# The first microseconds of an attention and experts block: silu from Exp, the first root on ScalarE, the upper halves ahead of the decay

## Chip, cores and metric

One core of one Trainium2 chip. The metric is the device time of one execution in microseconds (us), the median of several runs. A profiled execution gives the trace; its span goes from the first to the last instruction.

## The reference

`x` is 8 sequences of 256 tokens with 128 features. A modulation is computed from a condition `c` (8 x 128), and everything else is one attention and one mixture of experts:

```python
mod = (silu(c) @ wmod).reshape(8, 6, 1, 128)
sa, ca, ga, sb, cb, gb = mod[:, 0], ..., mod[:, 5]
h = layernorm(x) * (1 + ca) + sa
# attention: 16 heads of 8; the scores are multiplied by a decay before the softmax
lag = abs(i - j); scores = (q @ k.T) * scale * exp(-alpha * lag)
x = x + ga * (softmax(scores) @ v @ Wo.T + bo)
h = layernorm(x) * (1 + cb) + sb
# 16 experts, 2 per token, and one shared
x = x + gb * (routed_experts(h) + shared_expert(h))
```

The layer norm needs 1 / sqrt(variance + eps), silu is c / (1 + exp(-c)).

## The kernel before

The kernel is written for each engine by hand: five programs (SP for the loads, GpSimd, ScalarE, VectorE, TensorE) that run beside each other, each in its own written order, and meet only in semaphores. An engine does nothing behind a wait until that wait is over.

**Chunks.** The 2048 tokens are four chunks of 512 (two sequences each). Attention runs over the chunks one after the other, 32 head steps each in groups of four: TensorE makes scores from `qk_st` (L979), VectorE multiplies them with `decay` and takes the maximum (`head`, L736, L741), GpSimd forms maximum minus score (L306), TensorE turns it, ScalarE takes Exp (L420), and TensorE multiplies with the values in `v_one` (L1009). The experts follow, over the same four chunks, in units of two experts.

**Upper and lower halves.** Queries and keys are split into a rounded upper part and the remainder, and the four combinations of them lie in `qk_st`, which SP fills by copies from `qk` (`stack_slot`, L151, issued at L153), 64 in all. For the first four heads of the first chunk there is no time for copies: `w_first` has its rows arranged so that one matmul gives all combinations, ScalarE writes the upper halves to `act_hi` (`first_hi`, L562), and VectorE subtracts and writes `qk_st` directly (`first_lo`, L836).

**The start.** The first chunk is treated one sequence at a time. "First rows" are the two tiles of 128 tokens of the first sequence (tiles 0 and 1), "second rows" those of the second (tiles 2 and 3). The order of the work is:

- SP issues ten loads (`load`, L173 to L185): the first rows' `x_all`, `ct_sb` (the condition), `wmod_sb` for the first two modulations, the identity `id_f`, the second rows' `x_all`, `wf_sb`, `decay` (which holds the lags at first), the rest of `wmod_sb`, `wa_sb` (attention weights), and the rest of `x_all`. ScalarE issues three small ones (L547 to L549): `vf_sb`, `alpha_sb`, `vec_sb`.
- VectorE clears `attn_t`, on which TensorE runs warm-up matmuls (`warm`, L1160). It takes statistics and means of the first rows (`stats_first`, L819), normalises them to `xn` (`xn_first`, L829), copies the first two modulations out of PSUM (L853, L854), makes `nalpha` (L856), and does the statistics of the second rows. Then come `first_lo` for the first sequence, `xn` of the second rows, and three heads.
- GpSimd clears and marks the first half of `v_one` (`clear_values`, L330: one memset over all, two strided ones that put the 1.0 by which the sums are formed), then makes the root of the first rows, `(variance + eps) ** -0.5` (`root_first`, L324, L326 and L328), that of the second rows, the shift for later rows (`ln1_shift`), and, once the second rows' `xn` is done, the second half of `v_one`. After that its loop over the head steps begins.
- ScalarE takes silu of the condition (L551), loads the table set that holds Ln and Exp, runs an Exp on `spare` (L555), shifts and scales the transposed rows to `h_t` (`h_first`, L557), takes Exp of the lags (L578, in place in `decay`), and then the upper halves of the first sequence, the second sequence's `h_t`, and so on.
- TensorE runs eight warm-ups, the two modulations from `silu_c`, two more warm-ups, the transposes of `xn` (`lnt_first`), three warm-ups, the matmuls with `wf_sb` (`first`), four warm-ups, the scores, the second rows' transposes, and the projections with `wa_sb` (`project_seq`).

Two places show how a wait stands in front of a later one. ScalarE's order of the first sequence, and the load semaphore that both the lags and `alpha` count on:

```python
act_e.wait_ge(s["ld_decay"], 32)          # L576: lags and alpha, 16 each
act_e.wait_ge(s["nalpha_ok"], 1)
nc.scalar.activation(decay[:], decay[:], ACT.Exp, scale=nalpha[:, 0:1])
act_e.wait_ge(s["ld_vf"], 16)
first_hi(0)
```

VectorE waits for the same count of 32 ahead of `nalpha` (L855).

Of the kernel before, what the change touches and what calls it, by code (L numbers as in the profile page):

```python
# [50 lines left out]
def build(nc, x, x_t, c_t, w_first, v_first, w_attn, vecs, alpha, w_r, w_gu, w_d, w_mod, lag, ident, out):  # L51
# [3 lines left out]
    with ExitStack() as ctx:  # L55
        def sb(name, shape, dt=F32):
            return ctx.enter_context(nc.sbuf_tensor(name, shape, dt))

        def sem(name):
# [16 lines left out]
        wmod_sb = sb("wmod_sb", [P, 6, D])  # L76
        ct_sb, silu_c = sb("ct_sb", [P, NB]), sb("silu_c", [P, NB])
        mod_t = sb("mod_t", [P, 6, NB])
        gate_s, gate_m = sb("gate_s", [P, 2, NB]), sb("gate_m", [P, 2, NB])
        bo2, ga_bo = sb("bo2", [P, 1]), sb("ga_bo", [P, NB])  # L80
        nhalf, spare, eps = sb("nhalf", [P, TT]), sb("spare", [P, TT]), sb("eps", [P, 1])

# [43 lines left out]
        s = {n: sem(n) for n in (  # L126
            "ld_x0 ld_x0b ld_ct ld_id ld_vf ld_x xb_ok ld_mod ld_mod_b ld_first ld_attn ld_decay ld_ffn nalpha_ok decay_raw silu_ok modt_mm modt_ok modb_mm modb_ok "
            "stats_a mv_a vare_a rstd_a xn_a lnt_a h_a warm_ok first_mm first_hi first_ok bo_mm bo_ok gate_a gate_b gate_c gate_ok gabo_ok vone_ok pool_init eps_init lg_init whi_ok wlo_ok "
# [43 lines left out]
        def _(sp):  # L172
            def load(ap, dram, done):  # L173
                sp.dma_start(ap, dram).then_inc(s[done], 16)  # L174

            load(x_all[:, 0:BPC, :], x_v[:, 0:BPC, :], "ld_x0")
            load(ct_sb[:], c_t, "ld_ct")
            load(wmod_sb[:, SA:CA1 + 1, :], w_mod[:, SA:CA1 + 1, :], "ld_mod")
            load(id_f[:], ident, "ld_id")
            load(x_all[:, BPC:TT, :], x_v[:, BPC:TT, :], "ld_x0b")  # L180
            load(wf_sb[:], w_first, "ld_first")
            load(decay[:], lag, "ld_decay")
            load(wmod_sb[:, GA_IN:, :], w_mod[:, GA_IN:, :], "ld_mod_b")
            load(wa_sb[:], w_attn, "ld_attn")
            load(x_all[:, TT:, :], x_v[:, TT:, :], "ld_x")  # L185
# [84 lines left out]
        def _(pool):  # L270
# [11 lines left out]
            def ln1_shift(c):  # L282
                shift(c, mv, nmean, rstd, nmr, "mv_ok", "nmean_ok", "rstd_ok", "nmr_ok")
# [46 lines left out]
            def clear_values(k):  # L330
                nc.gpsimd.memset(v_one[:, k, :], 0.0).then_inc(s["pool_init"], 1)
                pool.wait_ge(s["pool_init"], 2 + k)
                cells = v_one[:, k, 0:TT * HEADS * VW].rearrange("p (t h a w) -> p t h a w", h=2, w=VW, t=TT)
                for h in range(2):
                    last = nc.gpsimd.memset(cells[:, :, h, :, VD + 1 - 2 * h:VD + 2 * HD - 2 * h:2], 1.0)
                last.then_inc(s["vone_ok"], 1)

            clear_values(0)
            root_first(slice(0, BPC), "mv_a", "vare_a", "rstd_a")
            root_first(slice(BPC, TT), "mv_ok", "vare_ok", "rstd_ok")  # L340
            ln1_shift(0)
            pool.wait_ge(s["xn_ok"], 1)
            clear_values(1)
            for i in range(NCHUNK):
# [15 lines left out]
        def _(act_e):  # L360
# [158 lines left out]
            def chunk(i):  # L519
                prev, nxt = i > 0, i < NCHUNK - 1  # L520
                for q in range(QUADS):
# [22 lines left out]
                    if (i, q) in SPLITS:  # L544
                        split(SPLITS.index((i, q)))

            act_e.dma_start(vf_sb[:], v_first).then_inc(s["ld_vf"], 16)  # L547
            act_e.dma_start(alpha_sb[:], alpha.to_broadcast([P, 1])).then_inc(s["ld_decay"], 16)
            act_e.dma_start(vec_sb[:], vecs).then_inc(s["ld_attn"], 16)  # L549
            act_e.wait_ge(s["ld_ct"], 16)  # L550
            nc.scalar.activation(silu_c[:], ct_sb[:], ACT.Silu).then_inc(s["silu_ok"], 1)  # L551
            act_e.wait_ge(s["pool_init"], 1)
            act_e.wait_ge(s["eps_init"], 1)
            nc.scalar.preload_act_table_set("natural_log_exp_and_others")
            nc.scalar.activation(spare[:], nhalf[:], ACT.Exp)  # L555

# [18 lines left out]
            h_first(0, "lnt_a", "h_a")  # L575
            act_e.wait_ge(s["ld_decay"], 32)  # L576
            act_e.wait_ge(s["nalpha_ok"], 1)
            nc.scalar.activation(decay[:], decay[:], ACT.Exp, scale=nalpha[:, 0:1]).then_inc(s["decay_raw"], 1)  # L578
            act_e.wait_ge(s["ld_vf"], 16)
            first_hi(0)  # L580
            h_first(1, "lnt_done", "h_ok")
# [59 lines left out]
        def _(dve):  # L641
# [174 lines left out]

            nc.vector.memset(attn_t[:], 0.0).then_inc(s["warm_ok"], 1)

# [23 lines left out]
            def qk_lo_seq(b, ready, done):  # L842
                for i in range(2):
# [4 lines left out]
                                                   ALU.subtract).then_inc(s[done], 1)  # L848

            stats_first(range(0, BPC), "ld_x0", "stats_a", "mv_a")  # L850
            xn_first(range(0, BPC), "rstd_a", "xn_a")
            dve.wait_ge(s["modt_mm"], 1)
            nc.vector.tensor_copy(mod_t[:, SA, :], ps_s[0][:, 0:NB]).then_inc(s["modt_ok"], 1)  # L853
            nc.vector.tensor_scalar(mod_t[:, CA1, :], ps_s[0][:, NB:2 * NB], 1.0, None, ALU.add).then_inc(s["modt_ok"], 1)  # L854
            dve.wait_ge(s["ld_decay"], 32)  # L855
            nc.vector.tensor_scalar(nalpha[:], alpha_sb[:], -1.0, None, ALU.mult).then_inc(s["nalpha_ok"], 1)  # L856
# [94 lines left out]
        def _(pe):  # L951
# [232 lines left out]

            warm(2)
            pe.wait_ge(s["ld_id"], 16)
# [143 lines left out]
```

## Time and profile before

| | |
|---|---|
| median of 3 runs | 238.72 us (238.61 to 238.99) |
| profiled execution | 238.33 us |
| its span | 236.5 us |
| instructions | 5820 |

The page counts busy time of each engine in the span, the chain that ended last by engine and line, and the load of the DMA engines. PE is TensorE's matmul, PEld its weight load, DVE is VectorE, ACT ScalarE, POOL GpSimd; an engine's name with a q is its queue of issues. All TensorE instructions have one line, L953, since a helper records them, so they are told apart by their operands.

### The profile page before, as it was taken

To read this page: it belongs to the slowest core of one execution; us is meant where nothing else is said; L and a number is where in the kernel's file an instruction comes from. 1 tells how busy PE (TensorE), PEld (TensorE's weight loads), DVE (VectorE), ACT (ScalarE), POOL (GpSimd) and SP (SyncE) were. 2 spreads that over 40 slices of the span, in tenths; PEclk is the share of its full clock that TensorE was granted. 3 is DMA by queue.
4 is the path that set the end of the run, shared out by engine and by line. 5 is a ranking of instruction groups with operands and counts; after the bars stand their busy time and mean duration, and the time that the engine had idled before them with its cause. 6 is when DMAs were issued, how large, how long until landed. Compare 5 with 4: busy or idle time off the path is not lost.

```text
span 236.5 us, 5820 instructions
## 1 busy us (share of the span) xinstructions
PE 225.0 (95%) x1828; PEld 166.0 (70%) x1828; DVE 189.9 (80%) x793; ACT 165.1 (70%) x335; POOL 181.5 (77%) x334
## 2 busy tenths in 40 slices
PE   7879999999999999999998999999999999999994
PEld 7767657665666676667666767677788887787882
DVE  3699897998998889899799988387756796966763
ACT  5558767699586999686975796776667659565550
POOL 6599898999897989989999989156486464666551
PEclk9999999999999999999999999999999999999999
DMA  5715845741008711017622540024323430045201
GB/s 143 225 46 123 245 162 136 198 113 47 4 15 198 186 63 36 0 29 198 176 81 96 196 136 0 4 91 133 111 81 127 127 98 0 0 135 198 95 26 44
DMA packets 16622, 24.38 MB, mean 103 GB/s; under 512 B 3344, under 2 KB 6544, under 8 KB 16464
## 3 DMA queue, kind: packets, MB, share of 16 engines
q1 hardware_dynamic: 16160, 24.01, 35.0%
q8 instruction: 15, 0.25, 0.4%
q14 instruction: 15, 0.12, 0.2%
q10 hardware_dynamic: 432, 0.01, 0.1%
HBM read 13.39 MB, written 1.18 MB: 62 GB/s over the span
## 4 chain that ended last, share of the span: by engine, by line
PE 61%; DVE 13%; ACT 11%; SPq 5%; issue 4%; DMA 3%; POOL 3%; DVEq 0%; ACTq 0%
PE bank L953 61%; DVE sc L741 5%; ACT pr L420 4%; SPq L153 4%; POOL sc L306 2%; ACT h_t L362 2%; DMA decay<-in_lag 1%; ACT xn L375 1%; DMA qk_st<-qk 1%; SPq L174 1%; DVE sc L917 1%; DVE qk_st L838 1%; DVE ex L702 1%; DVE mx L741 1%; DVE stats L644 1%
## 5 line engine op out<-in xcount | busy, mean ns | idle before, releaser
L306 POOL TENSOR_SCALAR sc<-sc,mx 128x256 f32<-128x256 f32 x256 | 121.3, 492 | 8.0 <-DVE mx L741 6.5
L741 DVE CUSTOM_DVE_ANT_0 sc<-bank,decay 128x256 f32<-128x256 f32 x256 | 91.0, 418 | 11.3 <-PE bank L953 11.1
L420 ACT ACTIVATE pr<-bank 128x512 f32<-128x512 f32 x128 | 69.2, 595 | 18.1 <-PE bank L953 18.1
L350 POOL TENSOR_TENSOR act_lo<-sc,act_hi 128x512 fp32r<-128x512 f32 x35 | 45.1, 1292 | 34.8 <-ACT act_hi L596 34.8
L953 PE MATMUL bank<-id_f,sc 128*128 128x128 f32 x512 | 69.1, 277 | 2.7 <-ACT pr L420 2.3
L953 PEld LDWEIGHTS bank<-id_f,sc 128*128 128x128 f32 x512 | 55.8, 141 | 16.4 <-issue 8.7
L911 DVE TENSOR_TENSOR pr<-bank,cwb 128x512 f32<-128x512 f32 x32 | 22.0, 688 | 15.6 <-PE bank L953 15.5
L953 PE MATMUL bank<-pr,v_one 128*32 128x256 f32 x512 | 34.3, 385 | 0.0
L605 ACT ACTIVATE bank<-bank 128x512 f32<-128x512 f32 x32 | 18.6, 582 | 20.5 <-PE bank L953 20.1
L917 DVE TENSOR_TENSOR sc<-pr,bank 128x512 f32<-128x512 f32 x36 | 24.7, 687 | 5.7 <-PE bank L953 2.4
L953 PE MATMUL bank<-h_hi,wgu_hi 128*128 128x512 f32 x72 | 28.8, 400 | 0.0
L953 PE MATMUL bank<-h_lo,wgu_hi 128*128 128x512 f32 x72 | 28.4, 395 | 0.0
L953 PE MATMUL bank<-h_hi,wgu_lo 128*128 128x512 f32 x72 | 28.4, 395 | 0.0
L596 ACT ACTIVATE act_hi<-sc 128x512 fp32r<-128x512 f32 x36 | 22.4, 623 | 2.9 <-DVE sc L917 2.9
L953 PEld LDWEIGHTS bank<-pr,v_one 128*32 128x32 f32 x512 | 13.3, 109 | 12.8 <-issue 4.9
L741 DVE DVE_READ_ACCUMULATOR2_ANT mx<- 128x1 f32 x256 | 21.0, 82 | 0.0
L953 PE MATMUL bank<-qk_st 32*128 32x256 f32 x256 | 16.2, 327 | 2.1 <-DVE mx L741 0.9
L953 PEld LDWEIGHTS bank<-h_hi,wgu_hi 128*128 128x128 f32 x72 | 13.5, 188 | 3.5 <-issue 0.4
L953 PEld LDWEIGHTS bank<-h_lo,wgu_hi 128*128 128x128 f32 x72 | 13.5, 187 | 3.3
L953 PEld LDWEIGHTS bank<-h_hi,wgu_lo 128*128 128x128 f32 x72 | 13.5, 188 | 3.1
L953 PEld LDWEIGHTS bank<-qk_st 32*128 32x128 f32 x256 | 9.8, 183 | 7.9 <-issue 5.8
L953 PE MATMUL bank<-act_hi,wd_hi 128*128 128x512 f32 x36 | 15.1, 419 | 0.0
(114 smaller groups left out, 267.2 us busy)
## 6 DMA issues: line engine op xcount, KB each, us to landing
cwb<-cw_dram SPq DMA_DIRECT2D x64, 128.0 KB, 3.0
qk_st<-qk SPq DMA_DIRECT2D x56, 128.0 KB, 2.7
wgu_sb<-in_w_gu SPq DMA_DIRECT2D x1, 1152.0 KB, 5.9
wgu_sb<-in_x_t SPq DMA_DIRECT2D x4, 256.0 KB, 3.8
x_all<-in_x SPq DMA_DIRECT2D x1, 768.0 KB, 6.0
o_sum<-o_t SPq DMA_DIRECT2D x6, 128.0 KB, 2.2
o_val<-o_t SPq DMA_DIRECT2D x6, 128.0 KB, 2.2
out_dram<-wgu_sb SPq DMA_DIRECT2D x3, 256.0 KB, 3.1
```

The source lines that it names most:

```text
L153: eng.dma_start(qk_st[slot:P:SLOTS, :, g, cols].bitcast(F32), qk[32 * g:32 * g + 32, bq:bk + 1:bk - bq, cols].bitcast(F32)).then_inc(done ...
L174: sp.dma_start(ap, dram).then_inc(s[done], 16)
L306: last = nc.gpsimd.tensor_scalar(sc[:, n % RING, t, :], sc[:, n % RING, t, :], -1.0, mx[:, n % RING, t:t + 1], ALU.mult, ALU.add)
L350: nc.gpsimd.tensor_tensor(act_lo[:, (i * NU + u) % FR, :], act[:, (i * NU + u) % FR, :], act_hi[:, (i * NU + u) % FR, :].bitcast(F32), ALU ...
L362: return nc.scalar.activation(dst, src, ACT.Identity, bias=bias[:, at:at + 1], scale=scale[:, at:at + 1])
L420: nc.scalar.activation(pr[:, n % RING, :, :].rearrange("p a b -> p (a b)"), turn_bank(i, n)[:], ACT.Exp, scale=-1.0).then_inc(s["exp_done" ...
L596: nc.scalar.activation(act_hi[:, (i * NU + u) % FR, :], act[:, (i * NU + u) % FR, :], ACT.Copy).then_inc(s["ahi_ok"], 1)
L605: nc.scalar.activation(gate[:], gate[:], ACT.Silu).then_inc(s["silu_done"], 1)
L741: last = nc.vector.tensor_tensor_reduce(sc[:, n % RING, t, :], ps_s[n % SB][:, t * SEQ:t * SEQ + SEQ], decay[:, t, :], float(HD) ** -0.5, ...
L911: nc.vector.tensor_tensor(gate_u[:, n % 2, :], up[:], cwb[:, u, :], ALU.mult).then_inc(s["mul_done"], 1)
L917: nc.vector.tensor_tensor(act[:, r, :], gate_u[:, n % 2, :], (gate if u < ROUTED else up)[:], ALU.mult).then_inc(s["act_ok"], 1)
L953: return nc.tensor.matmul(o, l, r, start=start, stop=stop, skip_group_check=not check, is_transpose=transpose or None)
```

## The change

Seven edits, all in the first part of the kernel:

- **silu from Exp.** ScalarE makes `c_den = exp(-c)`; VectorE adds 1, inverts and multiplies by `c` (`silu_of`, three small operations on 128 x 8 with a wait between each), between the first rows' means and their `xn`. The table set with Ln and Exp is loaded at the start; the load of the silu table and the Exp of `spare` at the start are gone.
- **The first rows' root** is made on ScalarE by Ln and Exp (`exp(-0.5 * ln(variance + eps))`).
- **GpSimd** marks `v_one` in a function of its own (`mark_sums`). It clears and marks the first half, waits for the first rows' `xn`, clears the second half, makes the second rows' root, marks the second half, and makes the shift.
- **Upper halves ahead of the decay** on ScalarE.
- **Loads.** `ct_sb` goes to ScalarE's queue, as its first; `vec_sb` to SP's; `wf_sb` goes ahead of the second rows' `x_all`, and `wa_sb` and `vec_sb` ahead of the rest of `wmod_sb`. ScalarE's other two loads come behind the table load in its program.
- **Waits.** `alpha` has a semaphore of its own, on which VectorE waits.
- **Warm-up.** `attn_t` is cleared over 128 of its 512 columns, and two warm-ups ahead of the transposes are gone.

```diff
             load(x_all[:, 0:BPC, :], x_v[:, 0:BPC, :], "ld_x0")
-            load(ct_sb[:], c_t, "ld_ct")
             load(wmod_sb[:, SA:CA1 + 1, :], w_mod[:, SA:CA1 + 1, :], "ld_mod")
             load(id_f[:], ident, "ld_id")
+            load(wf_sb[:], w_first, "ld_first")
             load(x_all[:, BPC:TT, :], x_v[:, BPC:TT, :], "ld_x0b")
-            load(wf_sb[:], w_first, "ld_first")
             load(decay[:], lag, "ld_decay")
+            load(wa_sb[:], w_attn, "ld_attn")
+            load(vec_sb[:], vecs, "ld_attn")
             load(wmod_sb[:, GA_IN:, :], w_mod[:, GA_IN:, :], "ld_mod_b")
-            load(wa_sb[:], w_attn, "ld_attn")
             load(x_all[:, TT:, :], x_v[:, TT:, :], "ld_x")
...
             def clear_values(k):
                 nc.gpsimd.memset(v_one[:, k, :], 0.0).then_inc(s["pool_init"], 1)
+
+            def mark_sums(k):
                 pool.wait_ge(s["pool_init"], 2 + k)
...
             clear_values(0)
-            root_first(slice(0, BPC), "mv_a", "vare_a", "rstd_a")
+            mark_sums(0)
+            pool.wait_ge(s["xn_a"], 1)
+            clear_values(1)
             root_first(slice(BPC, TT), "mv_ok", "vare_ok", "rstd_ok")
+            mark_sums(1)
             ln1_shift(0)
-            pool.wait_ge(s["xn_ok"], 1)
-            clear_values(1)
...
+            act_e.dma_start(ct_sb[:], c_t).then_inc(s["ld_ct"], 16)
+            nc.scalar.preload_act_table_set("natural_log_exp_and_others")
             act_e.dma_start(vf_sb[:], v_first).then_inc(s["ld_vf"], 16)
-            act_e.dma_start(alpha_sb[:], alpha.to_broadcast([P, 1])).then_inc(s["ld_decay"], 16)
-            act_e.dma_start(vec_sb[:], vecs).then_inc(s["ld_attn"], 16)
+            act_e.dma_start(alpha_sb[:], alpha.to_broadcast([P, 1])).then_inc(s["ld_alpha"], 16)
             act_e.wait_ge(s["ld_ct"], 16)
-            nc.scalar.activation(silu_c[:], ct_sb[:], ACT.Silu).then_inc(s["silu_ok"], 1)
-            act_e.wait_ge(s["pool_init"], 1)
+            nc.scalar.activation(c_den[:], ct_sb[:], ACT.Exp, scale=-1.0).then_inc(s["cexp_ok"], 1)
             act_e.wait_ge(s["eps_init"], 1)
-            nc.scalar.preload_act_table_set("natural_log_exp_and_others")
-            nc.scalar.activation(spare[:], nhalf[:], ACT.Exp)
+            act_e.wait_ge(s["mv_a"], 1)
+            nc.scalar.activation(var_e[:, 0:BPC], mv[:, 0:BPC, 1], ACT.Ln, bias=eps[:, 0:1], scale=1.0).then_inc(s["vare_a"], 1)
+            act_e.wait_ge(s["vare_a"], 1)
+            nc.scalar.activation(rstd[:, 0:BPC], var_e[:, 0:BPC], ACT.Exp, scale=-0.5).then_inc(s["rstd_a"], 1)
...
             h_first(0, "lnt_a", "h_a")
-            act_e.wait_ge(s["ld_decay"], 32)
+            act_e.wait_ge(s["ld_vf"], 16)
+            first_hi(0)
+            act_e.wait_ge(s["ld_decay"], 16)
             act_e.wait_ge(s["nalpha_ok"], 1)
             nc.scalar.activation(decay[:], decay[:], ACT.Exp, scale=nalpha[:, 0:1]).then_inc(s["decay_raw"], 1)
-            act_e.wait_ge(s["ld_vf"], 16)
-            first_hi(0)
             h_first(1, "lnt_done", "h_ok")
...
-            nc.vector.memset(attn_t[:], 0.0).then_inc(s["warm_ok"], 1)
+            nc.vector.memset(attn_t[:, 0:P], 0.0).then_inc(s["warm_ok"], 1)
...
+            def silu_of():
+                dve.wait_ge(s["cexp_ok"], 1)
+                nc.vector.tensor_scalar(c_den[:], c_den[:], 1.0, None, ALU.add).then_inc(s["cden_ok"], 1)
+                dve.wait_ge(s["cden_ok"], 1)
+                nc.vector.reciprocal(c_den[:], c_den[:]).then_inc(s["cinv_ok"], 1)
+                dve.wait_ge(s["cinv_ok"], 1)
+                nc.vector.tensor_tensor(silu_c[:], ct_sb[:], c_den[:], ALU.mult).then_inc(s["silu_ok"], 1)
+
             stats_first(range(0, BPC), "ld_x0", "stats_a", "mv_a")
+            silu_of()
             xn_first(range(0, BPC), "rstd_a", "xn_a")
...
-            dve.wait_ge(s["ld_decay"], 32)
+            dve.wait_ge(s["ld_alpha"], 16)
             nc.vector.tensor_scalar(nalpha[:], alpha_sb[:], -1.0, None, ALU.mult).then_inc(s["nalpha_ok"], 1)
...
-            warm(2)
             pe.wait_ge(s["ld_id"], 16)
             lnt_first(0, "xn_a", "lnt_a")
```

## Rows read from the trace of the kernel before

**Rows 1.** The page: granted clock in 40 slices, and the chain by engine.
```profile
PEclk9999999999999999999999999999999999999999
...
PE 61%; DVE 13%; ACT 11%; SPq 5%; issue 4%; DMA 3%; POOL 3%; DVEq 0%; ACTq 0%
```

**Rows 2.** The chain that ended last, in order of time: start us, us, what.
```profile
3.66 3.46 DMA decay<-in_lag
...
8.02 0.55 ACT act_hi L565
...
8.60 0.95 DVE qk_st L838 x2
...
24.46 2.79 DMA qk_st<-qk
```

**Rows 3.** Timeline, 1 to 6 us: start us, us, engine, line, operation, operands [idle before].
```profile
1.44 3.59 PE L953 MATMUL bank<-attn_t 128*128 128x128 f32 x16 [1.44 <-DVE attn_t L817]
...
2.14 1.28 ACT L551 ACT_TABLE_LOAD   x1 [2.14 <-issue]
...
2.78 0.65 POOL L335 MEMSET v_one<- 128x256 f32 x2
...
3.63 0.25 DVE L826 BATCH_NORM_AGGREGATE mv<-stats 128x2 f32<-128x6 f32 x2
...
3.99 0.21 ACT L551 ACTIVATE silu_c<-ct_sb 128x8 f32<-128x8 f32 x1 [0.56 <-DMA ct_sb<-in_c_t]
...
4.21 1.28 ACT L554 ACT_TABLE_LOAD   x1
4.25 0.73 POOL L328 TENSOR_TENSOR rstd<-var_e,nhalf 128x2 f32<-128x2 f32 x1
...
5.01 0.60 DVE L832 TENSOR_SCALAR xn<-x_all,mv,rstd 128x128 f32<-128x128 f32 x2 [1.13 <-POOL rstd L328]
...
5.51 0.20 ACT L555 ACTIVATE spare<-nhalf 128x4 f32<-128x4 f32 x1
```

**Rows 4.** The same timeline, 6 to 17 us.
```profile
6.27 0.56 ACT L362 ACTIVATE h_t<-bank,mod_t 128x256 f32<-128x256 f32 x1 [0.56 <-PE bank L953]
...
6.98 1.10 PE L953 MATMUL bank<-h_t,wf_sb 128*128 128x256 f32 x4
...
7.40 0.72 ACT L578 ACTIVATE decay<-decay,nalpha 128x512 f32<-128x512 f32 x1 [0.56 <-DVE nalpha L856]
...
8.07 0.19 POOL L326 TENSOR_SCALAR var_e<-mv 128x2 f32<-128x2 f32 x1 [3.09 <-DVE mv L826]
...
9.46 0.59 DVE L832 TENSOR_SCALAR xn<-x_all,mv,rstd 128x128 f32<-128x128 f32 x2
...
10.11 1.82 POOL L331 MEMSET v_one<- 128x2064 f32 x1 [0.51 <-DVE xn L832]
...
10.29 0.42 DVE L741 CUSTOM_DVE_ANT_0 sc<-bank,decay 128x256 f32<-128x256 f32 x1 [0.23 <-PE bank L953]
...
13.53 1.13 PE L953 MATMUL bank<-h_t,wa_sb 128*128 128x256 f32 x4 [1.20 <-DVE qk_st L838]
...
14.27 0.91 ACT L571 ACTIVATE qk<-bank,vec_sb 128x256 fp32r<-128x256 f32 x2 [1.31 <-PE bank L953]
...
16.51 0.94 POOL L306 TENSOR_SCALAR sc<-sc,mx 128x256 f32<-128x256 f32 x2 [0.23 <-DVE mx L741]
```

**Rows 5.** Three lines, each by itself: duration ns min/median/max, first and last start us.
```profile
L382 ACT ACTIVATE var_e<-mv,eps x6: 290/306/328, 20.0 to 136.6; 128x4 f32<-128x4 f32 x6
...
L723 DVE RECIPROCAL rz<-zs x2: 177/178/178, 104.0 to 135.3; 128x4 f32<-128x4 f32 x2
...
L888 DVE TENSOR_TENSOR gate_m<-mod_t,gate_s x1: 414/414/414, 23.2 to 23.2; 128x16 f32<-128x16 f32 x1
```

**Rows 6.** DMA issues of the first 25 us: KB each, us to landing.
```profile
x_all<-in_x SPq DMA_DIRECT2D x2, 128.0 KB, 2.5
...
alpha_sb<-in_alpha ACTq DMA_DIRECT2D x1, 0.5 KB, 2.6
```

More of the change, by code:

```diff
@@ L76, in build @@
         wmod_sb = sb("wmod_sb", [P, 6, D])
-        ct_sb, silu_c = sb("ct_sb", [P, NB]), sb("silu_c", [P, NB])
+        ct_sb, c_den, silu_c = sb("ct_sb", [P, NB]), sb("c_den", [P, NB]), sb("silu_c", [P, NB])
         mod_t = sb("mod_t", [P, 6, NB])
@@ L80, in build @@
         bo2, ga_bo = sb("bo2", [P, 1]), sb("ga_bo", [P, NB])
-        nhalf, spare, eps = sb("nhalf", [P, TT]), sb("spare", [P, TT]), sb("eps", [P, 1])
+        nhalf, eps = sb("nhalf", [P, TT]), sb("eps", [P, 1])
         x_all = sb("x_all", [P, NCHUNK * TT, D])
@@ L126, in build @@
         s = {n: sem(n) for n in (
-            "ld_x0 ld_x0b ld_ct ld_id ld_vf ld_x xb_ok ld_mod ld_mod_b ld_first ld_attn ld_decay ld_ffn nalpha_ok decay_raw silu_ok modt_mm modt_ok modb_mm modb_ok "
+            "ld_x0 ld_x0b ld_ct ld_alpha ld_id ld_vf ld_x xb_ok ld_mod ld_mod_b ld_first ld_attn ld_decay ld_ffn nalpha_ok decay_raw cexp_ok cden_ok cinv_ok silu_ok modt_mm modt_ok modb_mm modb_ok "
             "stats_a mv_a vare_a rstd_a xn_a lnt_a h_a warm_ok first_mm first_hi first_ok bo_mm bo_ok gate_a gate_b gate_c gate_ok gabo_ok vone_ok pool_init eps_init lg_init whi_ok wlo_ok "
```

## The prediction

> **What bounds the kernel now.** I read the page's chain first, to see which engine the time belongs to: 61% of the chain that ended last is TensorE's own work, at a granted clock that is full (2.4 GHz) in every one of the 40 slices [rows 1]. The change touches only the first 15 us or so, so the second view is the chain in order of time over the first 30 us [rows 2]. There the end is not set by TensorE: it runs through the landing of `decay` (issued 3.66, landed 7.12), the Exp of `decay` on ScalarE, the rounding to `act_hi` at 8.02, VectorE's two `qk_st` parts at 8.60 to 9.55, then (through the scores, the second rows' transposes, `h_t` and the rest of the second sequence) to a run of issues of `qk_st` copies on SP whose last one goes out at 24.46 and lands at 27.25. Behind that landing stands ScalarE's next `qk`, and from 28.66 TensorE itself is the chain. What is won ahead of 9.55 therefore moves the whole string, if each later link follows from the one before and not from something that stays put. Third, I read the timeline of each engine from 1 to 16 us, for what each instruction really waited for [rows 3, 4].
>
> **Part one: the first rows' root, and silu.** Before: VectorE's means end at 3.88 (3.63 + 0.25); GpSimd does the root in two instructions that end at 4.98, and VectorE starts `xn` at 5.01 [rows 3]. After: ScalarE does Ln and Exp. An Ln with its bias from memory takes 0.30 [rows 5], an Exp 0.20 (that of `spare`), and an engine follows its predecessor after some 0.03: 3.88 + 0.03 + 0.30 + 0.03 + 0.20 + 0.02 = 4.46. In VectorE's queue the three small operations of silu now stand ahead of `xn`. A small tensor_scalar or tensor_tensor isn't shown with GpSimd quiet and both operands in SBUF; from below I bound it by 0.15 (GpSimd's own 0.19 for the same size is near it), from above by the 0.41 that `gate_m` took beside a running GpSimd [rows 5]. Here GpSimd's marking has ended at 3.43 [rows 3], so I take 0.15, and 0.18 for the reciprocal [rows 5]: 3.91 + 0.15 + 0.03 + 0.18 + 0.03 + 0.15 = 4.45. The two strings end together, so `xn` starts at about 4.46 in place of 5.01: **0.55 earlier**. By the upper bound silu would end at 4.97 and this part would bring nearly nothing.
>
> Silu's input must be there. `ct_sb` moves to the head of ScalarE's queue (issue 0.72, in place of 1.23 on SP); ScalarE then has one table load of 1.28 and two issues of 0.45 before its Exp, which puts the Exp at 1.17 + 1.28 + 0.90 = 3.35 at the latest if nothing of this overlaps, and it ends by 3.6, ahead of 3.91. The second load of 1.28 (4.21 to 5.49) and the Exp of `spare` go, but ScalarE sat idle behind them until 6.27 [rows 3, 4], so they bring nothing by themselves: they are what allows ScalarE to do the root at all. The Trainium skill (ScalarE: Activation LUTs, section What ACT_TABLE_LOAD costs) adds a drain of about 1.38 us to each load of about 1.28. Here the Exp of `spare` started at 5.51, 0.02 after the load's end, so the trace shows no such drain; what it would cost is a rival below.
>
> Silu's result came at 4.20 and now comes at 4.45; TensorE was in its sixteen warm-up matmuls until 5.03 [rows 3], and with a clearing of `attn_t` a quarter as wide these start, and end, some 0.3 earlier. So the modulation's matmuls follow at about 4.55 and are done before `xn` is (5.06). They are covered; without the cover silu would show with 0.25. Two warm-up pairs of matmuls go ahead of the transposes; the wait there is for `xn`, so I cost their absence at nothing as long as the clock stays full, as it does now even across idle time [rows 1].
>
> **Part two: upper halves ahead of the decay.** Before, `h_t` began at 6.27; the matmuls with `wf_sb` began at 6.98; ScalarE took `decay` at 7.40 (it waited for the landing at 7.12) for 0.72 and could start `act_hi` only at 8.02 [rows 2, 4]. With `act_hi` first, its start is set by TensorE alone. The same pattern of matmuls with nothing in ScalarE's way stands at 13.53, with ScalarE's `qk` at 14.27: 0.74 from the first matmul to the taking [rows 4]. So 6.98 + 0.74 = 7.72 against 8.02: **0.30 earlier** by the swap alone. The matmuls need `wf_sb`, which is now issued two places earlier on SP, so it is no later. Together, `act_hi` starts at 8.02 - 0.55 - 0.30 = 7.17, and `qk_st` at 7.75 instead of 8.60: **0.85**.
>
> **What must not be late next.** `decay` now runs behind `act_hi`, at 8.17 to 8.89; VectorE's first head, which reads it, would start at 10.29 - 0.85 = 9.44, and ScalarE's second `h_t` later still, so 0.5 us of cover. Its load moves up one issue slot (about 0.5) with the same bytes ahead of it, so it lands between 6.6 and 7.12. The wait for `alpha` comes ahead of the second rows' statistics in VectorE's queue: issued at 1.65 or, behind the load, at 2.95, it takes 2.6 to land [rows 6] and so comes at 5.6 at the latest; before, that place waited until 7.12 for `decay`. The second `x_all` piece is issued at the same place as before, with `wf_sb` ahead of it instead of `ct_sb`: 2.67 + 2.5 = 5.2, and at most 0.6 more for the 124 KB extra at the rate of the rows before it. Statistics and means take 0.8, so means by 6.6.
>
> GpSimd: it waits for the first `xn` (5.06), clears for 1.82 (until 6.95), then var, 0.09 and the power, 0.19 + 0.09 + 0.73 [rows 3, 4]: the second root is ready at about 8.0. VectorE asks for it at 9.46 - 0.85 = 8.61, behind `qk_st`. Cover 0.6; beyond it each us of delay costs one. The marking (0.65) comes after it, next to VectorE's second `xn`. The queues: `vec_sb` goes from ScalarE's queue to SP's, and the attention weights pass the rest of the modulation's; they land near 8, and TensorE asks at 9.5. The modulation's rest lands about 0.5 later, some 7 us before it is used. The large `x_all` load keeps its place.
>
> GpSimd's second clearing, from 10.11 to 11.93, and its marking no longer stand ahead of the loop, so GpSimd's first head step can start near 10 instead of behind 12.5. I cost this at nothing: at 16.51 GpSimd had waited for VectorE [rows 4], so its lateness was made up by then.
>
> **Sum.** 0.55 + 0.30 = 0.85 off the chain. The profiled execution (238.33, span 236.5) would go to 237.48; it stands 0.39 below the median of the runs, so on the median 238.72 - 0.85 = 237.87, which I give as 237.9. A measurement of this kernel can tell about 0.2% (0.48 us) from no change.
>
> **Rivals.**
> *A, the gain is partly swallowed* (0.15). Silu's operations take the upper bound, or one link of the string to 27.25 hangs on something that stays put, such as the SP's issues being held by the DMA rings. For it: that string holds 16 copies, and the transfer of 2.79 is not TensorE's. Against: the copies' first wait is VectorE's result, which moves. With only part two left: 238.72 - 0.30 = 238.4.
> *B, the early GpSimd brings more* (0.05). If TensorE's first turns were held by GpSimd's late start rather than by VectorE, up to 0.5 more: 237.4.
> *C, ScalarE isn't ready* (0.03). If the first load blocked ScalarE for twice its 1.28, and the two issues came after, the Exp would run from 4.63 to 4.83, silu end at 5.40 and `xn` start at 5.41, 0.40 late; less the 0.30: 238.8. The drain rule of the Trainium skill quoted above would give 0.1 more than this. The start at 5.51 speaks against it.
> *D, slower: the second root comes late* (0.04). The place is GpSimd's clearing, now ahead of that root. It decides from 8.61 on, and the kernel is slower than before when the root passes 9.46. If the clearing were stretched beside VectorE as `gate_m` was (0.41 against 0.15, 2.7 times), it would take 4.9, the root would be ready at 11.1, and the time 238.72 + 1.65 = 240.4. Against: the clearing at 10.11 ran beside VectorE's heads and took the same 1.82 as the first.
> *E, the shifted start meets the long TensorE part badly* (0.03): the relative order of GpSimd and VectorE changes, up to 0.7 slower, 239.4. No row speaks for it.
>
> **How the numbers follow.** The forecast has 0.70: 237.5 to 238.2, nearly all of it faster by over 0.2%. Faster: 0.68 of it, B's 0.05, and 0.01 of A, 0.74. Same: the rest of A, C and 0.02 of the forecast, 0.19. Slower: D and E, 0.07. The range 237.1 to 238.6 leaves out D, E, C and the tails on both sides.
>
> **What would show it.** Right: one table load on ScalarE, Ln at about 3.9, `xn` at 4.4 to 4.6, `act_hi` at 7.1 to 7.3, `qk_st` at 7.7 to 7.8, the second `xn` near 8.6, the last first-chunk copy landing at 26.4, and every row behind it 0.85 earlier. Wrong: VectorE idle ahead of the second `xn` with GpSimd as releaser (D); the small operations at 0.3 or more each (A); a head that waits for `decay`; or a string that is 0.85 early at 10 us and on time at 27.

## The result and the profile after

| | before | after |
|---|---|---|
| median of 10 runs each | 238.74 us (238.23 to 239.53) | 237.81 us (237.45 to 238.48) |
| ratio | | 0.9958, 95% interval 0.9938 to 0.9978 |
| profiled execution, its span | 238.33, 236.5 | 237.55, 235.8 |

The change takes 0.93 us off the median; 0.85 was forecast. The whole interval lies beyond 0.2%. The sum came out, but not all of its terms did, so the profile after is read by its steps.

The page of the changed kernel, granted clock and chain (the answer to [rows 1]):

```profile
PEclk9999999999999999999999999999999999999999
...
PE 63%; DVE 13%; ACT 11%; SPq 4%; issue 3%; POOL 3%; DMA 1%; DVEq 0%; ACTq 0%
```

The timeline of the changed kernel, 1 to 10 us, rows of all engines in order of time (the answer to [rows 3, 4]):

```profile
1.04 3.78 PE L967 MATMUL bank<-attn_t 128*128 128x128 f32 x16 [1.04 <-DVE attn_t L822]
...
1.18 1.28 ACT L551 ACT_TABLE_LOAD   x1 [1.18 <-PEq L1336]
...
2.75 0.21 ACT L555 ACTIVATE c_den<-ct_sb 128x8 f32<-128x8 f32 x1 [0.29 <-DMA ct_sb<-in_c_t]
...
4.00 0.30 ACT L558 ACTIVATE var_e<-mv,eps 128x2 f32<-128x2 f32 x1 [1.04 <-DVE mv L831]
...
4.23 0.17 DVE L861 TENSOR_TENSOR silu_c<-ct_sb,c_den 128x8 f32<-128x8 f32 x1
...
4.51 0.93 PEld L967 LDWEIGHTS bank<-silu_c,wmod_sb 128*128 128x128 f32 x4
...
4.57 0.60 DVE L837 TENSOR_SCALAR xn<-x_all,mv,rstd 128x128 f32<-128x128 f32 x2 [0.17 <-ACT rstd L560]
...
5.22 1.82 POOL L331 MEMSET v_one<- 128x2064 f32 x1 [1.80 <-DVE xn L837]
...
5.39 0.49 PE L967 MATMUL bank<-id_f,xn 128*128 128x128 f32 x2
5.57 0.17 DVE L867 COPY mod_t<-bank 128x8 f32<-128x8 f32 x1 [0.41 <-PE bank L967]
...
5.98 0.56 ACT L365 ACTIVATE h_t<-bank,mod_t 128x256 f32<-128x256 f32 x1 [1.45 <-PE bank L967]
...
7.42 0.73 POOL L328 TENSOR_TENSOR rstd<-var_e,nhalf 128x2 f32<-128x2 f32 x1
7.46 1.02 ACT L570 ACTIVATE act_hi<-bank,vf_sb 128x256 fp32r<-128x256 f32 x2 [0.91 <-PE bank L967]
8.05 0.94 DVE L843 SCALAR_TENSOR_TENSOR qk_st<-bank,vf_sb,act_hi 128x256 fp32r<-128x256 f32 x2 [1.50 <-ACT act_hi L570]
8.37 0.71 ACT L585 ACTIVATE decay<-decay,nalpha 128x512 f32<-128x512 f32 x1
8.91 0.59 DVE L837 TENSOR_SCALAR xn<-x_all,mv,rstd 128x128 f32<-128x128 f32 x2
```

Two rows of the kernel before go beside these:

```profile
4.76 0.53 PEld L953 LDWEIGHTS bank<-silu_c,wmod_sb 128*128 128x128 f32 x4
...
5.76 0.41 PE L953 MATMUL bank<-id_f,xn 128*128 128x128 f32 x2
```

`xn` is 0.44 earlier, and `h_t` only 0.29. In between stand TensorE's matmuls for the modulation and its transposes of `xn`, and TensorE was still slow: the four weight loads for the modulation took 0.93, against 0.53 before, and VectorE's copy of the result waited 0.41 for them. But the modulation was not what `h_t` waited for. It was copied by 5.81, and the transposes ended at 5.88 (5.39 + 0.49), 0.10 ahead of `h_t`; before, they ended at 6.17, also 0.10 ahead. The transposes began only 0.37 earlier than before, 0.22 behind the end of `xn` in place of 0.14, while the modulation's last weight load ran until 5.44; and they took 0.49 in place of 0.41. `act_hi` is 0.56 earlier, `qk_st` 0.55.

The chain of the changed kernel in order of time (the answer to [rows 2]):

```profile
1.04 4.86 PE bank L967 x22
...
8.05 0.95 DVE qk_st L843 x2
...
24.01 2.91 DMA qk_st<-qk
```

`decay` has left the chain, and TensorE's own start, warm-up and modulations, has entered it. From `qk_st` on the string moved too, but less and less: 0.55 there, 0.45 at the last copy's issue (24.46 to 24.01), 0.33 at its landing (27.25 to 26.92). TensorE's last long piece began at 203.90 before and at 203.13 after, 0.77 earlier. Most of this extra arises far behind the change, at one instruction of VectorE. Before and after:

```profile
120.24 2.40 DVE L689 TENSOR_TENSOR h_lo<-h_t,h_hi 128x512 fp32r<-128x512 f32 x1
...
119.85 1.95 DVE L694 TENSOR_TENSOR h_lo<-h_t,h_hi 128x512 fp32r<-128x512 f32 x1
```

`h_lo`, a subtraction for the experts, starts 0.39 earlier and is 0.45 shorter; the head step behind it (122.56 and 121.90) is 0.66 earlier. The change does not touch this place. In the profiles of the twelve kernels below, `h_lo` took 1.50 to 2.07 in ten and 2.41 and 2.51 in two, e12 and e8, both with the new root. So it differs by profile and isn't shown to be a gain of the change. The last 0.1 appears near 157.

### The profile page after: what moved, and what is told of

Same layout as the page of the kernel before. It is cut to its first block, busy times and chain, and to the rows that moved or that the text cites. A ratio compares the mean times of both kernels' runs of the same rounds, so it can differ in the third digit from the quotient of the medians.

```text
span 235.8 us, 5813 instructions
## 1 busy us (share of the span) xinstructions
PE 224.9 (95%) x1824; PEld 166.1 (70%) x1824; DVE 189.5 (80%) x796; ACT 164.0 (70%) x335; POOL 180.6 (77%) x332
## 3 DMA queue, kind: packets, MB, share of 16 engines
q1 hardware_dynamic: 16160, 24.01, 35.7%
## 4 chain that ended last, share of the span: by engine, by line
PE 63%; DVE 13%; ACT 11%; SPq 4%; issue 3%; POOL 3%; DMA 1%; DVEq 0%; ACTq 0%
PE bank L967 63%; DVE sc L746 6%; ACT pr L423 4%; SPq L153 4%; POOL sc L306 2%; ACT h_t L365 2%; ACT xn L378 1%; DMA qk_st<-qk 1%; DVE sc L931 1%; DVE qk_st L843 1%; DVE ex L707 1%; DVE mx L746 1%; DVE stats L649 1%; DVE struck L719 1%; ACT L610 1%
## 5 line engine op out<-in xcount | busy, mean ns | idle before, releaser
L967 PEld LDWEIGHTS bank<-id_f,sc 128*128 128x128 f32 x512 | 55.7, 141 | 16.8 <-issue 8.7
```

The lines of the kernel that those rows point to most:

```text
L967: return nc.tensor.matmul(o, l, r, start=start, stop=stop, skip_group_check=not check, is_transpose=transpose or None)
```

## The experiments

Twelve kernels ran, four at a time on one chip, in 12 executions each. The table gives each against the kernel before on the same chip (medians of different chips are not compared) and, in us of its one profile, the start of `h_t`, `act_hi` and `qk_st` and the last tenth of a us in which the TensorE weight loads under way still took about 300 ns or more on average.

| kernel | median | ratio to before (95%) | range | `h_t`, `act_hi`, `qk_st` | slow until |
|---|---|---|---|---|---|
| e0_after | 237.59 | 0.9966 (0.9951 to 0.9981) | 237.27 to 238.39 | 6.10, 7.58, 8.18 | 5.8 |
| e1_decay_first | 237.86 | 0.9966 (0.9952 to 0.998) | 237.3 to 238.22 | 5.77, 7.74, 8.32 | 3.8 |
| e2_swap_only | 238.66 | 1.0002 (0.9987 to 1.0017) | 238.01 to 239.32 | 6.53, 8.01, 9.04 | 5.1 |
| e3_root_on_gpsimd | 238.55 | 0.9999 (0.9981 to 1.0017) | 237.73 to 239.22 | 6.62, 8.73, 9.33 | 10.2 |
| e7_old_warmup | 239.08 | 0.9999 (0.9981 to 1.0018) | 237.67 to 239.55 | 6.10, 7.58, 8.18 | 4.2 |
| e9_gpsimd_root_warm | 239.05 | 1.0012 (0.9988 to 1.0035) | 237.89 to 240.43 | 6.61, 8.09, 8.69 | 5.7 |
| e4_clear_twice | 239.46 | 1.0036 (1.0013 to 1.0059) | 238.93 to 244.27 | 6.16, 7.88, 8.48 | 7.0 |
| e8_qk_behind_exps | 237.86 | 0.9961 (0.9947 to 0.9975) | 237.52 to 238.26 | 6.09, 7.57, 8.17 | 5.9 |
| e11_full_clearing | 237.91 | 0.9968 (0.995 to 0.9985) | 237.31 to 238.54 | 6.38, 7.86, 8.46 | 5.8 |
| e12_two_warmups | 238.17 | 0.9994 (0.9972 to 1.0015) | 237.43 to 239.94 | 6.21, 7.69, 8.29 | 4.9 |
| e13_new_warmup_only | 238.48 | 1.0 (0.998 to 1.0019) | 237.81 to 239.82 | 6.29, 8.13, 8.71 | 5.3 |
| e14_old_warmup_again | 238.32 | 0.9998 (0.9983 to 1.0014) | 237.69 to 239.21 | 6.39, 7.87, 8.47 | 4.9 |

The kernel before had medians of 238.55, 238.9 and 238.57 on the three chips, with executions from 237.84 to 239.73.

### First four: the changed kernel again, the swap, the root

> The changed kernel itself, once more, beside the others. Theory 1 (TensorE's own clock): its first matmuls run at half speed until a moment that varies from execution to execution; in the first profile of the changed kernel the weight loads took 333 ns until about 5.3 us, so that the two modulations took 0.93 us in place of 0.51 and h_t came at 5.98 in place of 5.72. Then this execution need not show the same: with the rise at 4.7 or earlier h_t is at 5.7, with the rise at 5.3 it is at 5.98 again. Theory 2 (the earlier warm-up brought the modulations into the slow stretch, always): h_t at 5.98 again, the rise at 5.3. Time 237.8 by both.

Inconclusive between the two theories by itself: TensorE rose at 5.8, later still, and `h_t` came at 6.10. Here the slow stretch reached through the transposes:

```profile
5.34 0.67 PE L967 MATMUL bank<-id_f,xn 128*128 128x128 f32 x2
```

The kernel e1 has the same start on TensorE and decided it: there the loads took 192 ns from 4.1 on.

```diff
 h_first(0, "lnt_a", "h_a")
+act_e.wait_ge(s["ld_decay"], 16)
+act_e.wait_ge(s["nalpha_ok"], 1)
+nc.scalar.activation(decay[:], decay[:], ACT.Exp, ...)
 act_e.wait_ge(s["ld_vf"], 16)
 first_hi(0)
-act_e.wait_ge(s["ld_decay"], 16)
-act_e.wait_ge(s["nalpha_ok"], 1)
-nc.scalar.activation(decay[:], decay[:], ACT.Exp, ...)
```

> The changed kernel with the Exp of decay put back ahead of the upper halves, all else as changed. Theory (the order on ScalarE is worth what decay's landing makes of it): decay landed at 7.45 in the changed kernel, so its Exp starts near 7.5 and act_hi near 8.1 in place of 7.46: 0.65 later, 238.4 to 238.5. Rival (the swap is worth the 0.30 of the prediction, the rest is the root): 0.3 later, 238.1.

The timeline of e1_decay_first, TensorE and ScalarE:

```profile
4.46 0.52 PEld L967 LDWEIGHTS bank<-silu_c,wmod_sb 128*128 128x128 f32 x4 [0.19 <-issue]
...
5.26 0.41 PE L967 MATMUL bank<-id_f,xn 128*128 128x128 f32 x2 [0.19 <-DVE xn L837]
...
5.77 0.56 ACT L365 ACTIVATE h_t<-bank,mod_t 128x256 f32<-128x256 f32 x1 [1.29 <-PE bank L967]
7.11 0.72 ACT L583 ACTIVATE decay<-decay,nalpha 128x512 f32<-128x512 f32 x1 [0.77 <-DMA decay<-in_lag]
7.74 1.00 ACT L570 ACTIVATE act_hi<-bank,vf_sb 128x256 fp32r<-128x256 f32 x2
```

With TensorE fast the four loads take 0.52, the transposes 0.41, and `h_t` starts at 5.77, where the prediction had 5.72. Against e0, with `xn` at 4.52 in both, that is 0.33 earlier: 0.08 by the transposes' start and 0.26 by their own length. So Theory 1 holds: the earlier start doesn't always put the modulations into the slow stretch. From `h_t` to `act_hi` it is 1.97 here, 1.48 in the changed kernel, 1.75 before: the order on ScalarE is worth 0.3 to 0.5 in a profile, depending on when `decay` lands. In the medians undoing it cost 0.27, the rival's figure, and the ratio is the same, 0.9966. What the swap brings to the median is not settled beyond "between nothing and 0.3".

```diff
 # kernel before
 h_first(0, "lnt_a", "h_a")
+act_e.wait_ge(s["ld_vf"], 16)
+first_hi(0)
 act_e.wait_ge(s["ld_decay"], 32)
 act_e.wait_ge(s["nalpha_ok"], 1)
 nc.scalar.activation(decay[:], decay[:], ACT.Exp, ...)
-act_e.wait_ge(s["ld_vf"], 16)
-first_hi(0)
```

> The kernel before with the upper halves put ahead of the Exp of decay, nothing else. Theory: act_hi at 7.72 (6.98 + 0.74) in place of 8.02, every later row 0.30 earlier, 238.74 - 0.30 = 238.4. Rival (decay, now late, holds VectorE's first head): the head at 10.29 unchanged, 238.7.

The time is the rival's (1.0002; the lower end of the interval, 0.9987, would be the theory's 0.30), its mechanism is not: the first head came at 10.74, 0.45 later than before, and `decay` had been ready since 9.64. VectorE's timeline in e2_swap_only:

```profile
8.29 0.15 DVE L856 TENSOR_SCALAR nalpha<-alpha_sb 128x1 f32<-128x1 f32 x1 [2.35 <-DMA decay<-in_lag]
8.36 0.48 DVE L822 BATCH_NORM_STATS2 stats<-x_all 128x6 f32<-128x128 f32 x2
8.87 0.25 DVE L826 BATCH_NORM_AGGREGATE mv<-stats 128x2 f32<-128x6 f32 x2
9.04 0.84 DVE L838 SCALAR_TENSOR_TENSOR qk_st<-bank,vf_sb,act_hi 128x256 fp32r<-128x256 f32 x2
```

ScalarE began `act_hi` at 8.01, so `qk_st` could have started at 8.6. VectorE still stood at the count of 32, which `alpha` and the lags share; the lags landed at 8.27, and statistics and means stood in between. Freeing one queue from a landing moved the wait to the next queue. This is one execution, with a late landing and with TensorE slow until 5.1 (`h_t` 0.26 later than before). In the profile of the kernel before the lags landed at 7.12 and VectorE's means were done at 7.98, so the same wait would not have held `qk_st`, which by the rows of after would start at 8.34 (6.27 + 1.48 + 0.59, an estimate). A semaphore of its own for `alpha` takes this wait away; the prediction told of it as cover and gave it no price, and it was not tried alone.

```diff
 # changed kernel
 mark_sums(0)                                              # GpSimd
+root_first(slice(0, BPC), "mv_a", "vare_a", "rstd_a")
...
-act_e.wait_ge(s["mv_a"], 1)                               # ScalarE: Ln and Exp of the root
-nc.scalar.activation(var_e[:, 0:BPC], ..., ACT.Ln, ...)
-act_e.wait_ge(s["vare_a"], 1)
-nc.scalar.activation(rstd[:, 0:BPC], ..., ACT.Exp, scale=-0.5)
```

> The changed kernel with the first rows' root back on GpSimd (var and power ahead of its wait for xn), silu still from Exp, all else as changed. Theory: rstd at 5.0, xn at 5.03 in place of 4.57, and h_t at 6.25 to 6.3 whatever TensorE's speed: 0.3 to 0.5 later than the changed kernel, 238.1 to 238.3. Rival (TensorE's modulations and not xn set h_t, so the root on ScalarE brings nothing): h_t within 0.1 of the changed kernel's, 237.8.

`xn` came at 5.09, as expected, but the whole lead was gone, more than the theory's 0.3 to 0.5. TensorE's weight loads in e3_root_on_gpsimd:

```profile
5.80 0.29 PEld L964 LDWEIGHTS bank<-id_f,xn 128*128 128x128 f32 x2 [0.32 <-issue]
6.08 1.40 PEld L964 LDWEIGHTS bank<-attn_t 128*128 128x128 f32 x6
7.36 1.40 PEld L964 LDWEIGHTS bank<-h_t,wf_sb 128*128 128x128 f32 x4
8.85 1.78 PEld L964 LDWEIGHTS bank<-attn_t 128*128 128x128 f32 x8
```

The last three groups took 0.75, 0.73 and 1.08 in the changed kernel. TensorE was slow until 10.2, `act_hi` came at 8.73, and this execution took 239.08, in the upper half of its kernel's twelve. The lowest of the twelve, 237.73, stands 0.46 above the changed kernel's lowest on that chip (237.27), close to the 0.52 by which `xn` is later here.

### Second four: the warm-up, the cover, the string of copies

```diff
 # changed kernel, e7_old_warmup and e14_old_warmup_again
-nc.vector.memset(attn_t[:, 0:P], 0.0)
+nc.vector.memset(attn_t[:], 0.0)
...
+warm(2)
 pe.wait_ge(s["ld_id"], 16)
 lnt_first(0, "xn_a", "lnt_a")
```

> The changed kernel with the warm-up of before: all of attn_t cleared, two more warm-ups ahead of the first transposes. Theory (the moment at which TensorE goes from half to full speed varies by execution and the warm-up only shifts its chances): the first matmul at 1.44, the modulations at about 4.9; h_t between 5.7 and 6.3 depending on the rise; median within 0.3 of the changed kernel's 237.6 to 237.8. Rival (the early, light modulations delay the rise): with the heavier warm-up the rise comes by 4.8 as in the kernel before, h_t at 5.75, and the median is 0.2 to 0.3 below the changed kernel's.

Both wrong: with the old warm-up the changed kernel has no lead at all (0.9999). Its one profile fell on the lowest of its twelve executions (237.67), where `qk_st` came at 8.18, so the profile doesn't show the loss: its `h_t`, `act_hi` and `qk_st` are those of e0_after to 0.01. Against e8, the changed kernel's start on the same chip, the median is 1.22 higher and the lowest execution only 0.15.

```diff
 # e3_root_on_gpsimd, e9_gpsimd_root_warm
+warm(2)
 pe.wait_ge(s["ld_id"], 16)
 lnt_first(0, "xn_a", "lnt_a")
```

> The kernel with the first root back on GpSimd (238.55, no faster than before, its profile with TensorE at half speed until 10.3 us) and, in addition, the two warm-ups ahead of the transposes restored. Theory (there xn came at 5.7 with TensorE idle since 5.5 after light matmuls, and that gap let it stay at half speed): with the gap filled the rise comes by 6 and the median falls to 238.1 to 238.3, the 0.46 of the root above the changed kernel. Rival (the gap has nothing to do with it, the root on ScalarE is worth all of it by another way): 238.5 again.

The theory fell; by the ratio it is the rival's case. The rise was at 5.7 in the profile, but the time did not fall: 1.0012, with two groups, 237.89 to 238.64 and 239.45 to 240.43. A filled gap on TensorE did not help.

```diff
 # changed kernel, e4_clear_twice
 pool.wait_ge(s["xn_a"], 1)
+nc.gpsimd.memset(v_one[:, 1, :], 0.0).then_inc(s["twice_ok"], 1)
+pool.wait_ge(s["twice_ok"], 1)
 clear_values(1)
```

> The changed kernel with GpSimd's second clearing done twice (1.82 us more ahead of the second root). Theory of the cover (0.6 predicted; in the changed kernel's profile the root was ready at 8.15 and VectorE asked for it at 8.91): the root is ready at about 10.0, xn of the second rows starts at 10.0 in place of 8.91, the rest follows 1.1 later: 238.7 to 238.9. Rival (the second rows have slack further down, because SP's copies of the second sequence are issued one after the other anyway): 238.0 or less.

VectorE in e4_clear_twice:

```profile
10.07 0.70 DVE L839 TENSOR_SCALAR xn<-x_all,mv,rstd 128x128 f32<-128x128 f32 x2 [0.65 <-POOL rstd L328]
```

The root was ready at 10.03 and `xn` of the second rows 1.16 later than in the changed kernel. Of this, 0.43 is a slower TensorE in this execution (`qk_st` at 8.48 in place of 8.05), and 0.7 is the root, for which VectorE waited 0.65. The theory holds for the place: of the added 1.82 a part was covered, and the rest went to the end. The median of 239.46 lies above its 238.7 to 238.9. TensorE's last long piece began at 204.51, 1.38 after the changed kernel's. The ratio is 0.7% above the changed kernel's, more than that, and the profile, one of the two fastest of its twelve, doesn't show the rest. Rival D's place is thus real, and the cover kept it away: ready at 8.15, asked for at 8.91.

```diff
 # changed kernel, e8_qk_behind_exps: the first qk of the second chunk
-if q == 3 and nxt:
+if q == 3 and nxt and i:
     qk_hi_of(i + 1, 0, ps_m)
...
     exps(i, q - 1, 1)
+if q == 3 and i == 0:
+    qk_hi_of(1, 0, ps_m)
```

> The changed kernel with one more edit, past the start: ScalarE takes the next chunk's first qk, which waits for the last of the first chunk's copies (landing at 26.92), behind the two Exps of its place instead of ahead of them. Theory (the string of copies sets the end until 28.3 and ScalarE's wait of 1.58 passes it on to TensorE): the Exps run at about 26.6 in place of 27.59, TensorE's wait of 0.69 at 28.32 goes, and the kernel gains 0.4 to 0.8: 237.0 to 237.3. Rival (TensorE's next projection waits for that qk one group later, so the time only moves): 237.6 to 237.8, unchanged.

TensorE in e8_qk_behind_exps:

```profile
27.67 1.09 PE L969 MATMUL bank<-id_f,sc 128*128 128x128 f32 x8
...
31.47 0.51 PE L969 MATMUL bank<-qk_st 32*128 32x256 f32 x8 [0.68 <-DVE mx L748]
```

and the same two places in e0_after:

```profile
28.42 1.12 PE L967 MATMUL bank<-id_f,sc 128*128 128x128 f32 x8 [0.65 <-ACT pr L423]
...
31.49 0.51 PE L967 MATMUL bank<-qk_st 32*128 32x256 f32 x8
```

TensorE gained 0.75 at 28 and had lost it at 31.5, where it waits for VectorE's maximum. The rival holds in its result (0.9961, no gain). The chain showed SP's copies because they came last there, but VectorE was just behind, so the string to 27 is not the only bound.

### Last four: which part of the warm-up

```diff
 # changed kernel, e11_full_clearing
-nc.vector.memset(attn_t[:, 0:P], 0.0)
+nc.vector.memset(attn_t[:], 0.0)
```

> The changed kernel with all of attn_t cleared (the warm-up starts at 1.44 in place of 1.04), no warm-ups added. With the whole old warm-up put back the changed kernel lost its lead (239.08 against 238.90 before on that chip, executions from 237.67 to 239.55 in two groups). Theory (the start of the warm-up decides when TensorE rises to full speed): this part alone loses it again, ratio to before 0.998 to 1.001, two groups. Rival (the two warm-ups decide, or the rise is chance): ratio 0.996 as the changed kernel.

The rival holds: 0.9968. The later start is seen (`h_t` at 6.38) and doesn't take the lead away.

```diff
 # changed kernel, e12_two_warmups
+warm(2)
 pe.wait_ge(s["ld_id"], 16)
```

> The changed kernel with the two warm-ups ahead of the first transposes restored, clearing as changed. Theory (the two warm-ups stand in front of the transposes on TensorE, whose xn is ready at 5.17, so they delay h_t by their 0.4 to 0.8 when TensorE is still at half speed): h_t at 6.4 to 6.6 in such a profile, median 0.3 to 0.6 above the changed kernel, ratio 0.998 to 0.999. Rival (they are covered by the wait for xn, as the prediction had it): ratio 0.996.

The lead goes: 0.9994 (the interval, 0.9972 to 1.0015, still touches that of e11). `h_t` at 6.21 is below the 6.4 to 6.6 of the theory, which held for a slow TensorE. TensorE in e12_two_warmups:

```profile
4.62 0.74 PE L967 MATMUL bank<-silu_c,wmod_sb 128*128 128x8 f32 x4
5.21 0.69 PE L967 MATMUL bank<-attn_t 128*128 128x128 f32 x4
5.73 0.38 PE L967 MATMUL bank<-id_f,xn 128*128 128x128 f32 x2
```

`xn` was ready at 5.14, and the two warm-ups stood in front of the transposes, which began 0.34 after those of the changed kernel (5.39) although TensorE was fast from 5.0 on. Where it is slow the four loads of the two warm-ups take 0.81 in place of 0.53, as in e9. In the kernel before their loads ended at 5.73, 0.11 behind the end of `xn` (5.62), and in e13, without them, the transposes' loads began 0.12 behind it: there they cost nothing.

The profile also shows how much else moves. This execution took 238.52, in the upper half of its twelve and 0.85 above that of e0_after; its first `qk_st` is only 0.11 later. The rest arises behind the start. The longest issue in SP's string, ScalarE's wait for the string's end, and `h_lo`, in e0_after:

```profile
20.05 1.35 SPq L153
...
27.10 0.69 ACT L399 ACTIVATE qk<-bank,vec_sb 128x512 fp32r<-128x512 f32 x1 [1.54 <-DMA qk_st<-qk]
...
119.96 1.96 DVE L694 TENSOR_TENSOR h_lo<-h_t,h_hi 128x512 fp32r<-128x512 f32 x1
```

and in e12_two_warmups:

```profile
20.16 1.81 SPq L153
...
27.66 0.69 ACT L399 ACTIVATE qk<-bank,vec_sb 128x512 fp32r<-128x512 f32 x1 [2.00 <-DMA qk_st<-qk]
...
120.53 2.41 DVE L694 TENSOR_TENSOR h_lo<-h_t,h_hi 128x512 fp32r<-128x512 f32 x1
```

At 20 us 0.46 was lost in the issue of one copy, and at 120 us 0.3 in `h_lo`. No row ties either to the two warm-ups. Nor does the start of the other profiles show their price: e7 (with them, TensorE slow until 4.2) has `h_t` at 6.10 like e0 (without them, slow until 5.8), and e14 has 6.39 beside e11's 6.38.

```diff
 # kernel before, e13_new_warmup_only
-nc.vector.memset(attn_t[:], 0.0)
+nc.vector.memset(attn_t[:, 0:P], 0.0)
...
-warm(2)
 pe.wait_ge(s["ld_id"], 16)
```

> The kernel before with the changed warm-up alone: 128 columns of attn_t cleared, the two warm-ups gone. Theory (much of the change's gain in the median is the warm-up's): ratio 0.997 to 0.998. Rival (without the earlier root xn comes at 5.6 as before and TensorE waits for it in any case, so the warm-up brings nothing there, or leaves a gap in which TensorE stays at half speed): ratio 1.000 or above.

The rival holds: 1.0000. Without the early root TensorE waits for `xn` (transposes at 5.78 against 5.76 before).

The last is e7_old_warmup again, word for word.

> The kernel with the old warm-up once more, for a second profile: the first one fell on the fastest of its twelve executions (237.67) and had TensorE at full speed from 4.5. Theory (the slow group, 239.0 to 239.5, are executions in which TensorE stays at half speed past the first matmuls, to 7 or 10 us): a profile from the slow group shows weight loads of 333 ns past 6 us and qk_st later than 8.6. Rival (the slow group comes from something after the start): qk_st at 8.2 again, and the lost 1.2 us at a later place that the timeline names.

The ratio repeats (0.9998), but the profile fell on 237.87, again near the lower end, so neither theory is shown by it. On the same chip the median is 0.41 above e11's, the lowest execution 0.38. The transposes' loads began at 5.80, `h_t` at 6.39.

## Why the prediction was right, and where not

**The root on ScalarE: right.** Forecast `xn` at 4.46, measured 4.57 and 4.52 (Ln began 0.10 behind the means, where the sum had 0.03); silu ended at 4.40, forecast 4.45. The table load and the issues ran beside each other, and the first Exp started at 2.75, at the landing of `ct_sb`; the drain of about 1.38 which the Trainium skill (ScalarE: Activation LUTs, section What ACT_TABLE_LOAD costs) adds to a load would have put it at 3.84 or later, so the trace again shows none.

**TensorE's first matmuls at full speed: wrong in most profiles.** The step read the warm-up's end (5.03 in the one profile of before) as TensorE being ready and priced the matmuls at what they took there. TensorE's first microseconds have two speeds, and the place of the rise differs by execution: 3.8 to 7.0 in the profiles that share the changed kernel's start and early root, 10.2 in e3. The modulations, said to be covered, then last until 5.5 and put the transposes' first matmul some 0.08 later, and the transposes themselves take 0.49 to 0.67 instead of 0.41. `h_t` comes at 5.98 to 6.16 instead of 5.72. The root's 0.55 shrank to 0.29 on the profile's path.

**The swap: right in the profile** (0.27 from `h_t` to `act_hi`, forecast 0.30), unsettled in the median. The lags' landing was forecast at 6.6 to 7.12 and came at 7.46. In all profiles it came between 6.6 and 7.6 when issued at 3.15 (eleven) and at 7.12, 7.23 and 8.27 when issued at 3.66 (three): it differs more from profile to profile than by the issue.

**The two warm-ups "at nothing": the step that failed.** "The wait there is for `xn`" was true of the kernel before, where they ended as `xn` came. With `xn` 0.44 earlier that cover was gone, and the edit became part of the gain: that much the medians show. The four kernels with the early root and without the two warm-ups (e0, e1, e8, e11) stand at 0.9961 to 0.9968, the changed kernel's first runs at 0.9958; the three with the early root and the warm-ups at 0.9994 to 0.9999; root on GpSimd without warm-ups, and warm-ups gone from the kernel before, at 0.9999 and 1.0000. Neither half brings anything alone that the ratios show. This leaves out e4, whose extra clearing is a loss of its own, and e9, with neither half, at 1.0012. How the warm-ups cost as much as the medians say is not shown: by the lowest executions on the same chip it is 0.12 to 0.38, about what a delay of the transposes can give (0.34 in e12's profile), by the medians 0.26 to 1.22. Of the three, e12's interval (from 0.9972) overlaps e11's (to 0.9985) widely.

**The sum** was near the result partly by chance. The profile gives 0.55 at `qk_st` for the forecast 0.85 (at 8.05, forecast 7.75) and 0.33 at the last copy's landing (at 26.92, forecast 26.4). In the middle half of the executions on one chip the changed kernel runs from 237.55 to 237.85 and the kernel before from 238.10 to 238.85, so that it leads by 0.55 at the lower edge and by 1.00 at the upper: its executions spread less. That upper half was in no step. Two profiles of slow executions point to two different places: e3's (239.08) had TensorE slow until 10.2, e12's (238.52) lost its time at 20 and 120 us. Which of them makes the upper half, and why the changed kernel has less of it, stays open.

**The rivals.** A was partly true. 0.85 became 0.55 by TensorE, not by silu, whose small operations took 0.14 to 0.20; and 0.55 became 0.33 in SP's string, the place A named: its longest issue took 1.44 after 1.36, its last transfer 2.91 after 2.79. From the first copy's issue to the last one's landing the fourteen profiles took 14.8 to 15.9, so 0.2 more or less there need not be the change's. B didn't show: GpSimd's first head step moved from 12.60 to 10.62 and had to wait 1.32 for VectorE even so; nothing came of it. C and D did not happen; D's mechanism was shown by e4. E left no sign.

Not tried: the order of the loads, GpSimd's old order and `alpha`'s semaphore, each undone alone.

## What to carry to other kernels

When an input comes earlier, price everything that stands in front of its reader in the queue again, filler work above all: what ended just in time before can be a delay now. When a landing leaves one engine's way, look for the next queue that counts on the same semaphore. Where the gain is a few tenths of a us at the start, one profile isn't the distribution: compare the lower and the upper executions, undo the parts singly and in pairs, and compare two profiles row by row to the end, since a part of their difference can arise where nothing was changed.

## What the hardware showed

- The granted clock reads 1.00 (2.4 GHz) in every slice from the start, yet the same weight load of 128 x 128 took 333 ns in TensorE's first microseconds and 192 ns later, 1.7 times as long. The durations point to the lower level (1.2 GHz), the column doesn't show it. The Trainium skill (TensorE: Matmul & The Clock Gate, Part 1: The HAM clock gate) says that TensorE starts at 1.2 GHz and that the number of slow matmuls varies from run to run; the rises at 3.8 to 10.2 agree.
- The start of the warm-up alone doesn't set the rise: with the first matmul at 1.04 it came at 3.8 to 10.2 (nine profiles), with the first at 1.44 at 4.2 to 5.8 (five).
- The same load of 256 KB, issued at 3.15 to 3.67, landed between 6.6 and 8.3, with the DMA engines 60 to 100% busy from 3 to 7 us in the profiles of before, after and e0. A wait on it costs another time in each profile.
- In SP's string of sixteen copies the first issue took 0.76 to 0.78 and the others 0.61 to 0.64, except that in every profile one or two of the last eleven took longer, 0.71 to 1.81, at a place between 16.8 and 24.6 us that differs by profile.
- The same subtraction on VectorE (`h_lo`, 128 x 512, near 120 us) took 1.50 in one profile, 1.95 to 2.07 in ten and 2.40 to 2.51 in three. Three, four and five of GpSimd's instructions on `sc` ran beside it; why their number differs stays open.
